# SiLU of a mixture-of-experts stage made from tanh: one ScalarE tanh and one more VectorE product per step

## The reference, cut to what matters

```python
t = t + _L3_attn_ref(_ln_t(t), L3_attn_W, L3_attn_b)
t = t + _L3_ffn_ref(_ln_t(t), ...)
# in _L3_ffn_ref, D = 128, F = 64, 16 experts, 6 of them per token, 2 shared ones:
shared_out = einsum(silu(hg) * hu, shared_w_down) / 2
topk_p, topk_i = top_k(softmax(x @ router_w.T + bias), 6)
expert_out = einsum(silu(hg) * hu, w_down)      # hg, hu: gate and up products of an expert
sparse = segment_sum(gate_score * expert_out)   # by token
return shared_out + sparse
```

## Time and profile before

| | |
|---|---|
| three runs, us | 5563.34, 5563.64, 5557.48 (median 5563.34) |
| profiled execution: span from first to last instruction, us | 5548.6 |
| its own time outside the span | not listed; the runs lie 8.9 to 15.0 us above this span |
| last stage alone (its steps run from 4018 us on) | about 1530 us |
| PE, DVE, ACT, POOL busy over the span | 87%, 65%, 54%, 18% |
| mean granted TensorE clock | 0.952 of 2.4 GHz |
| one image of the last stage (from one last addition of attention to the next) | 100.65 us |

### The profile page before, as it was taken

How to read it: one execution, slowest core, us unless ns; L and a number is a source line. 1 busy time by engine, 2 the same in 40 slices (tenths; PEclk the granted TensorE clock), 3 DMA queues, 4 the chain that set the end, 5 groups by cost and what they waited for, 6 DMA issues and landing times.

```text
span 5548.6 us, 81822 instructions
## 1 busy us (share of the span) xinstructions
PE 4842.2 (87%) x25633; PEld 2616.5 (47%) x25633; DVE 3586.2 (65%) x7699; ACT 2987.7 (54%) x5420; POOL 1021.9 (18%) x1348
## 2 busy tenths in 40 slices
PE   5888888888888886957888888888899999999999
PEld 1222222222222221336777877787755555555554
DVE  6677777777777762555665656555576676766765
ACT  2655565665655653414555555556755455455552
POOL 2212112121222112202333333333210000000000
PEclk7999999999999998979999999999999999999999
DMA  2522222222222211223545454544321111111112
GB/s 84 144 70 81 81 70 70 70 73 78 73 89 82 66 45 38 29 68 106 165 140 163 141 162 147 157 146 129 106 61 45 50 48 45 50 46 47 52 45 75
DMA packets 406297, 477.10 MB, mean 86 GB/s; under 512 B 87640, under 2 KB 249648, under 8 KB 403760
## 3 DMA queue, kind: packets, MB, share of 16 engines
q1 hardware_dynamic: 372128, 424.84, 25.4%
q0 software_dynamic: 20576, 35.55, 2.3%
q10 hardware_dynamic: 13168, 11.48, 0.8%
HBM read 308.54 MB, written 145.57 MB: 82 GB/s over the span
## 4 chain that ended last, share of the span: by engine, by line
PE 33%; DVE 15%; issue 3%; DVEq 3%; ACT 2%; ACTq 0%; SPq 0%; DMA 0%
PE n_ps_f L2153 4%; PE n_ps_f L2146 4%; PE n_ps_xy L1801 3%; PE n_ps_h L1791 3%; PE n_ps_c L2193 2%; PE n_ps_h L2205 2%; PE n_ps_f L2140 2%; PE n_ps_f L1649 2%; PE n_ps_xy L2209 1%; DVEq L2025 1%; DVE n_stats L971 1%; DVE n_xln L983 1%; PE n_ps_f L995 1%; PE n_ps_h L2209 1%; DVE n_down_weights L2024 1%
## 5 line engine op out<-in xcount | busy, mean ns | idle before, releaser
L597 ACT ACTIVATE a_probs<-ps_b 128x512 f32<-128x512 f32 x2048 | 1111.0, 594 | 794.8 <-PE ps_b L693 782.0
L454 DVE TENSOR_REDUCE a_negmax<-ps_a 128x1 f32<-128x1024 f32 x1024 | 1206.1, 1219 | 378.9 <-PE ps_a L637 369.3
L637 PE MATMUL ps_a<-a_k_stack,a_q_stack 96*128 96x512 bf16 x2048 | 634.6, 396 | 178.8 <-DVE a_negmax L454 89.9
L693 PE MATMUL ps_b<-a_q_stack,a_k_stack 99*128 99x512 bf16 x2048 | 673.6, 391 | 68.2 <-ACT a_probs L597 30.9
L1604 ACT ACTIVATE n_hidden<-n_ps_h,n_b 128x128 f32<-128x128 f32 x1472 | 420.2, 374 | 339.1 <-PE n_ps_h L1791 338.3
L706 PE MATMUL ps_o<-a_probs,a_v_ones 128*32 128x512 f32 x4096 | 562.0, 622 | 0.2 <-ACT a_probs L597 0.2
L637 PEld LDWEIGHTS ps_a<-a_k_stack,a_q_stack 96*128 96x128 bf16 x2048 | 146.1, 99 | 732.2 <-DVE a_negmax L454 468.9
L1801 PE MATMUL n_ps_xy<-n_down_weights,n_hidden 128*128 x2944 | 410.7, 284 | 78.9 <-ACT n_xy L1618 72.8
L693 PEld LDWEIGHTS ps_b<-a_q_stack,a_k_stack 99*128 99x128 bf16 x2048 | 196.2, 100 | 487.8 <-ACT a_probs L597 251.5
L1801 PEld LDWEIGHTS n_ps_xy<-n_down_weights,n_hidden 128*128 128x128 f32 x2944 | 369.1, 196 | 117.0 <-issue 112.8
L1791 PE MATMUL n_ps_h<-n_xy,n_up_weights 128*128 128x128 f32 x2944 | 399.8, 279 | 3.6 <-issue 1.8
(11 more groups left out here) (346 smaller groups left out, 7532.8 us busy)
## 6 DMA issues: line engine op xcount, KB each, us to landing
n_up_weights<-in_L_ffn_W_dram SPq DMA_DIRECT2D x368, 256.0 KB, 2.7
n_up_weights<-score_scratch SPq DMA_DIRECT2D x512, 128.0 KB, 2.9
split_scratch<-a_pieces SPq DMA_DIRECT2D x180, 256.0 KB
a_q_stack<-split_scratch SPq DMA_DIRECT2D x128, 192.0 KB, 3.7
a_k_stack<-split_scratch SPq DMA_DIRECT2D x128, 192.0 KB, 4.1
rows_scratch<-n_zero SPq DMA_DIRECT2D x16, 1472.0 KB, 10.5
outs_scratch<-n_xy SPq DMA_DIRECT2D x176, 128.0 KB, 1.9
n_xg<-rows_scratch SPq DMA_DIRECT2D x80, 256.0 KB
```

The lines of the kernel that those rows point to most:

```text
L454: dve.tensor_reduce(negmax[:, b, t:t + 1], bank, axis=AX.X, op=ALU.max, negate=True).then_inc(ring_read, 1)
L597: act.activation(probs[:, m % PROBS, 512 * k:512 * k + 512], ps_b[:, k, :], ACT.Exp).then_inc(b_exp, 1)
L637: last = pe.matmul(bank[:, cols], q_stack[0:KS, h, 128 * t:128 * t + 128], k_stack[0:KS, h, cols], start=True, stop=True)
L693: pe.matmul(ps_b[:, k, :], k_stack[:, h, 128 * t:128 * t + 128], q_stack[:, h, 512 * k:512 * k + 512], start=True, stop=True).then_inc(b_u ...
```

## The change

ACT makes tanh(g / 2) in place of SiLU(g). DVE then makes (tanh + 1) times g, reading g from PSUM, which is twice the SiLU; the factor one half goes into the product with the scores (0.5) and, for the shared unit, from 0.5 to 0.25. PE waits with the next gate product until DVE has read `ps_g` (semaphore g_read), where it waited for ACT.

```diff
 # DVE, slot 3n+1
-                    dve.wait_ge(silu_up, i * STEPS + n + 1)
+                    dve.wait_ge(tanh_up, i * STEPS + n + 1)
+                    dve.scalar_tensor_tensor(act_up[:, n % 2, :], act_up[:, n % 2, :], 1.0, ps_g[:, :], ALU.add, ALU.mult).then_inc(g_read, 1)
+                    dve.drain()
                     dve.wait_ge(u_ps, i * STEPS + n + 1)
...
-                        dve.scalar_tensor_tensor(mixed[(i * STEPS + n) % 3], act_up[:, n % 2, :], 0.5, ps_u[n % 2][:, :], ALU.mult, ALU.mult).then_inc(u_read, 1)
+                        dve.scalar_tensor_tensor(mixed[(i * STEPS + n) % 3], act_up[:, n % 2, :], 0.25, ps_u[n % 2][:, :], ALU.mult, ALU.mult).then_inc(u_read, 1)
...
 # DVE, slot 3n+2
-                    dve.tensor_tensor(mixed[(i * STEPS + n) % 3], act_up[:, n % 2, :], scores[:, unit % RING, :], ALU.mult).then_inc(mixed_up, 1)
+                    dve.scalar_tensor_tensor(mixed[(i * STEPS + n) % 3], act_up[:, n % 2, :], 0.5, scores[:, unit % RING, :], ALU.mult, ALU.mult).then_inc(mixed_up, 1)
 # ACT, slot 3n
-                    act.activation(act_up[:, n % 2, :], ps_g[:, :], ACT.Silu).then_inc(silu_up, 1)
+                    act.activation(act_up[:, n % 2, :], ps_g[:, :], ACT.Tanh, scale=0.5).then_inc(tanh_up, 1)
 # PE, slot 3n
-                        pe.wait_ge(silu_up, i * STEPS + n)
+                        pe.wait_ge(g_read, i * STEPS + n)
```

More of the change, by code:

```diff
@@ L1879, in dense_attention_and_silu @@
     attention_in, choice_in, ffn_in, result_ps, result_up = (sem(x) for x in "attention_in choice_in ffn_in result_ps result_up".split())
-    g_ps, u_ps, silu_up, u_read, mixed_up, score_stored = (sem(x) for x in "g_ps u_ps silu_up u_read mixed_up score_stored".split())
+    g_ps, u_ps, tanh_up, g_read, u_read, mixed_up, score_stored = (sem(x) for x in "g_ps u_ps tanh_up g_read u_read mixed_up score_stored".split())
     scores_in = [sem(f"scores_in{n}") for n in range(RING)]
```

## The result

The changed kernel takes 5681.14 us (median of 4 runs, 5660.33 to 5686.47); the kernel before took 5563.49 beside it. The ratio is 1.0205, 95% interval 1.0186 to 1.0225: slower, as forecast (5675, range 5630 to 5715). The profiled execution has a span of 5658.5 us. Its stages ahead of the last one, whose code is unchanged, took 4004.8 us up to the first gate product of the last stage, 13.3 less than in the profile before, so I compare the last stage alone: 1653.7 us against 1530.5, which is 123.2 more. One image, from one last addition to the next, takes 109.39 us in the mean of the 13 images between the first and the last of these additions; before it took 101.20.

The account below looks back on a forecast made before the run. PE was taken to bound the attention stretch, DVE the norm and gate stretches. 3.7 + 2.6 + 1.3 = 7.6 us per image over 14 images, plus 4.1 and 2 for the last two, gave 112 us: 5675 us, range 5630 to 5715.

Parts of the forecast that it names:

- What bounds the kernel: Last stage: PE bounds the attention stretch, DVE the norm and gate stretches; one ACT load per image is on the path.
- The added product: DVE, every step: one 128x512 product with a PSUM operand, 0.68 us, 0.77 of the queue; changed factors cost nothing.
- The sum: Whole kernel: 7.6 us per image for 14 images, with the last two 112 us together, giving 5675 us.
- The moved wait: PE's g(n+1) waits for DVE's product of step n: one step of lead instead of two.
- Norm stretch: Stretch of 14.93 us per image where DVE decides: +3.7 us, g(15) starting at about 4317.8 instead of 4313.56.
- the ring of 2.54: Time from one gate product to the next through ACT and DVE: 2.54 us, where it was 1.82 through ACT alone.
- Gate stretch: Stretch of 28.94 us per image where DVE decides: +2.6 us, with tanh(2) ending 0.5 us earlier than SiLU(2) did.
- first rival: Loads stay because tanh lies in another table set: 15 x 0.7 = 10 us more, 5685; chance 0.05.
- Attention stretch: Stretch of 56.78 us per image that PE bounds: +1.3 us, 0.8 at step 8 and 0.5 at step 6.
- the forecast's 4.1 and 2: Last two images: image 14 pays 4.1 us, 4.6 for six DVE-bound steps less 0.5; image 15 pays 2 us.
- The second: Rival: the added product is dearer than 0.77 us; at 1.1 us, 4 us per image, 5731; chance 0.05.
- The third: Rival: faster, only ACT's path counts; 15 images gain 1.3 us each from the missing load, 5543; chance 0.05.

Follow-up runs that it names:

- e10: e3 with the u product of step 5 made three times instead of once in images 1 to 15, keeping PE busy: ratio 0.9980 to the kernel before.
- e11: The kernel before with the change in steps 6 to 13 of each image only: ratio 1.0031 to the kernel before.
- e12: The kernel before with the change in steps 0 to 5 and 14 to 17 only: ratio 1.0169 to the kernel before.
- e1: The kernel before with only PE's gate-product wait moved to DVE's product; SiLU stays, no added product: ratio 1.0140 to the kernel before.
- e2: The changed kernel with PE's wait back on ACT; the added product reads tanh twice, factor g left out: ratio 1.0216 to the kernel before.
- e9: The changed kernel with the u product of step 14 made five times instead of once in images 1 to 15: 5689.9 us, ratio 1.0231.
- e3: The kernel before with tanh in SiLU's place and nothing else, factor g left out: ratio 1.0013 to the kernel before.
- e4: The changed kernel with SiLU in tanh's place, so the table loads stay: ratio 1.0247 to the kernel before.
- e5: The kernel before with the product with the scores of images 1 to 15 made by GpSimd instead of DVE: ratio 1.0120.

## Why the prediction was right

- **What bounds the kernel.** It held. ACT lost 255 of 256 loads and the attention stretch got no shorter. e10 gained 0.2% from their absence; e11 and e12 show that the price is paid where the earlier trace rows have DVE as the bound.
- **The added product.** 681 ns against 0.68, and 0.78 of the queue against 0.77 (4330.91 to 4331.69). (Without a drain the next operation starts 0.61 us behind, not 0.68: line 2031 at 4321.54 and the next product at 4322.15 in the kernel before. The sum doesn't use it.) The factor in the product with the scores cost nothing: 688 ns in both kernels. Tanh takes 0.60 us, as SiLU did.
- **The moved wait.** It is real (e1) and its place is the norm stretch. The forecast walked both through the timeline together and did not add their prices; e1 and e2 show that adding them would have given some 13 us per image.
- **Norm stretch.** Put at 3.7, measured 4.46: the largest mis-sized term. The sum left the fall of the clock behind g(15) to its upper bound, and it did fall; e9 gives it 0.52 us of the 0.76. The trace shows the same place: between the added products of steps 15 and 16 lie 3.07 us (4330.91 to 4333.98) where the ring of 2.54 was forecast, and 2.53 in e9. The rest, 0.24, belongs to the image shown: inside its norm DVE stands 0.40 us for nothing that the profile shows, where it stood 0.07 before, so that the added product of step 14 starts 6.73 us behind the last addition instead of 6.49. In the mean of the 13 images the stretch is 4.11 us longer, and 3.58 in e9.
- **Gate stretch.** Put at 2.6, measured 2.84. The part for the load, 0.5, was right in the kernel before (e3, e10: 0.47); in the changed kernel its absence is worth 1.3 us of the gate stretch shown (e4), or 0.8 of the mean image, as in the forecast's first rival (0.7).
- **Attention stretch.** Put at 1.3, measured 1.17. The forecast had 0.8 at step 8 and 0.5 at step 6. At step 8 PE's wait for DVE went from 0.75 us to 1.20, which is 0.45; at the second tile there is a new one of 0.33 (4378.48). The other 0.4 is busy time of PE (56.12 against 55.74), so the sum came out nearer than its parts.
- **The sum.** 112 us for the last stage against 123.2 in the two profiles (117.7 between the medians). The 13 images took 8.19 us more each instead of 7.6, 7.7 us of the difference; the images at the end took 10.0, where a norm stretch and the forecast's 4.1 and 2 make 9.8; the first image 6.7 instead of the 3.9 without a norm stretch, and why was not tried.
- **The rivals.** The loads went, so the first falls. With one load left, the trace agrees with the Trainium skill, "ScalarE: Activation LUTs", section on table sets: tanh and exp share a set. The second falls by the 0.78 us; the rule of "VectorE: DVE Perf Modes" (the Trainium skill, section on the DRAIN) would give 1.09, and the trace disagrees with it here. The third falls by the sign. The ring in image 15 is 2.53 us (gate products at 5607.28 and 5609.81), put at 2.54.

## What to carry to other kernels

Before work is moved from an engine with idle time to another, cut the profile into stretches and price the work in each by the engine that bounds it: here the same change cost about 0.14 us a step in the stretch that PE bounds (1.1 over 8) and 0.67 in the two that DVE bounds (6.65 over 10). Loads that take 328 us of an engine were worth 0.2% of the time when they went (e10), and nothing that could be measured until PE's clock was kept up (e3). A wait that is moved from one engine to another and work added on the latter are walked through one timeline together, since their prices overlap.

## What the runs showed of the hardware that I had not expected

**Work taken off one engine can lower another's clock.** In e3 ACT was done sooner, PE ran ahead and paused 2.00 us instead of 1.03, and the scores behind the pause took 3.43 us at 1.2 GHz instead of 1.88. In e10 four added matmuls just ahead kept the clock at 2.4 GHz in 12 of 13 images, in seven of them behind a pause of 1.8 us or more: more work for PE made the kernel faster than e3. The length of the pause alone doesn't tell what the clock will do; two images of e3 kept it at 1.99 us. The same cure at g(15) (e9) gave 0.5 us in the norm stretch, where DVE was the bound, and 0.18 us in the mean image.

**GpSimd and DVE got in each other's way.** Beside GpSimd's products three of the gate's four two-input operations from SBUF grew by 0.9 to 1.1 us, while products with one input from PSUM kept 680 ns. The Trainium skill, "SBUF — State Buffer", section "Who interferes with whom", says that a DVE instruction with two SBUF inputs contends with a GpSimd instruction that reads SBUF, that one with at most one doesn't outside the 2-port modes, and that whichever of the two issues later is blocked. The trace of e5 agrees on both sides: DVE's line 1022 began at 4357.26 and kept its 2.28 us, and GpSimd's product at 4357.42 took 3.25 us where most took 1.27; DVE's next, line 1023, began at 4359.46 beside it and took 3.35. A tensor_scalar of DVE with one SBUF input grew as well (line 1033, 128x128, 227 to 1336 ns in the mean); whether it runs in such a mode no run here shows.
